# A Mamba scan between two expert layers: sum of state 14 one step earlier on TensorE, low parts of the projected rows one state later on VectorE

## The chip, the cores and the metric

The kernel runs on one core of a Trainium2 chip. The metric is the device time of one execution in microseconds; lower is better. Five engines work side by side, each through its own list of instructions in order: TensorE (PE; its weight loads are shown as PEld), VectorE (DVE), ScalarE (ACT), GpSimd (POOL) and SyncE (SP, which only starts transfers). They meet through semaphores.

## The reference

A block of three layers on x of 32 sequences x 256 tokens x 128 values, in float32: a mixture of 8 experts (two chosen for each token), a two-way Mamba layer, and the mixture again. The Mamba layer is the part that matters here. It is computed once forward and once on the flipped sequence, with weights of its own:

```python
xz = x @ in_w.T
xi, z = split(xz, 2)                       # 256 channels each
xc = silu(conv1d_depthwise(xi, 4 taps) + conv_b)
x_dbl = xc @ xp_w.T                        # dt (8), B (16), C (16)
delta = softplus(dt @ dtp_w.T + dtp_b)
# for each of 16 states n, over time t:
h[n] = h[n] * exp(delta * A[n]) + (delta * xc) * B[n]
y = sum over n of h[n] * C[n] + xc * Dp
out = (y * silu(z)) @ out_w.T
```

## The kernel before

The first expert layer (`moe(0)`), the Mamba stage and the second expert layer (`moe(1)`) follow one another. The Mamba stage is cut into 16 pairs `p` of two sequences each. A pair has two units: r=0 forward and r=1 backward; unit number u = 2p + r. A unit works on 256 channels (two halves c of 128 partitions) x 512 columns (2 sequences x 256 tokens), and on 16 states n, one after another. Each engine has a loop over the 16 states with the work of a state, and beside it, at fixed places of its list, the preparation of the next unit and the end of the one before. These places are tables at the top of the file: `DVE_AT`, `POOL_AT`, `ACT_AT`, `PE_AT`, `CONV_AT`, `SUM_AT`, keyed by the state at which the engine is. A whole number is behind that state's own work, a half one after the item of the whole number.

For each state n of a unit:

- ACT makes the decay exp(delta * A[n]) (`decay`, L1164; `decay_to_bank`, L1174, for the states 3, 9 and 15), three states ahead.
- The product delta * xc * B[n] comes from one of three ways. For the states 3, 9 and 15 POOL makes it (`product`, L535); for 2, 4, 6, 8, 10, 12 and 14 ACT scales a transposed copy (`scale_by_B`, L1197) and PE turns it back (`turn_back`, L1522); for 0, 1, 5, 7, 11 and 13 PE spreads the row B[n] over all partitions (`spread`, L1489) and DVE multiplies (`product`, L889).
- DVE runs the recurrence (`scan`: L917, or L904 for 3, 9 and 15).
- POOL multiplies with C[n] (`times_C`, L548) into one of four buffers `hC`. State N waits there until PE has summed state N - 4.
- PE adds the result to the unit's sum in banks 4 and 5 (`sum_states`, L1547, eight transposing matmuls), which ends by raising `y_done`.

When all 16 sums are done, DVE multiplies with silu(z) (`gate`, L877); `gate` waits for `y_done` of state 15. It stands behind the scan of state 2 of the next unit (`DVE_AT["gate"] = 2`).

`SUM_AT` says at which step of PE a state is summed; keys from 16 on are steps 0, 1, 2 of the next unit. Before, key 18 holds the states 14 and 15. `CONV_AT` puts the taps of the next unit's convolution (L1422) between: one tap of c=1 at 1.6 and two at 2.0, which stand ahead of the sums of step 2.

PE's list at step n is: turn back state n + 1, spreads, the items of n, the sums of n, a spread, the items of n + 0.5 and n + 0.6.

The preparation of the next unit goes: convolution (PE), silu (ACT, L1125), projection of z (PE, L1432), projection to dt, B and C into bank 6 (PE, `project_x`, L1454, at 4.5), their high parts (ACT, `split_hi`, L1135, at 3.5) and their low parts (DVE, `split_lo`, L864), rows that make float32 out of two shortened numbers; then the step size (PE, `project_dt`, L1465, at 8.5). `split_lo` waits for the high parts. `project_dt` and the spread of state 0 of the next unit wait for the low parts. Before, `DVE_AT["lo"]` is 5.5: behind the scan of state 5.

```python
def split_lo(p, r):
    dve.wait_ge(s["act_pre"], done(ACT_PRE, f"hi{r}", p))
    V.tensor_tensor(BCs[r][LOW:ROWS, :], bank[6][LOW:ROWS, :], ...)
def gate(u, r):
    dve.wait_ge(s["y_done"], (u + 1) * NS)
```

Of the kernel before, what the change touches and what calls it, by code (L numbers as in the profile page):

```python
# [39 lines left out]
ACT_NORM = ["xn", "xnT", "xnTrev"]  # L40


DVE_AT = {"stats": 2.5, "gate": 2, "sum": 5.5, "lo": 5.5, "size": 10.5}
POOL_AT = {"rstd": 1, "du": 9}
ACT_AT = {"xn": 3.0, "silus": 2.0, "xnT": 6.5, "hi": 3.5, "BT": 8.0, "parts": 8.5, "ln": 9.0, "gT": 12.0,
    "duT0": 12.5, "duT1": 14.5, "res": 13.5}
PE_AT = {"z": 3.0, "skip": 4, "xdbl": 4.5, "xt": 6.0, "BT": 8.0, "dt": 8.5, "gT": 11.5, "out0": 12.5,
    "out1": 12.5, "duT0": 12.5, "duT1": 14.0}
CONV_AT = {0.0: (0, 3, 1), 0.6: (1, 0, 1), 1.6: (1, 1, 1), 2.0: (1, 2, 2), 14.0: (0, 0, 2), 15.0: (0, 2, 1)}
SUM_AT = {6: (0, 1, 2), 7: (3, 4), 9: (5, 6), 11: (7, 8), 12: (9,), 13: (10,), 15: (11,), 16: (12, 13), 18: (14,  # L50
    15)}
SP_AT = {"rows": 8}
EARLY, Y_BUFS = 10, 3

# [70 lines left out]
def macaron_kernel(nc, x, gateT, wgT, wuT, wdT, inT, xpT, dtpT, chan, outT, ident, tri, e_rank,  # L125
# [38 lines left out]
    with ExitStack() as ctx:  # L164
# [414 lines left out]
        def _(dve):  # L579
# [268 lines left out]
            def layernorm(p):  # L848
                wait(dve, s["act_norm"], done(ACT_NORM, "xn", p - 1))
                dve.wait_ge(s["comb_done"], p + 1)  # L850
                dve.sem_inc(s["aggr_turn"], 1)
                for t in range(G):
                    ins = V.bn_stats(st[:, t, :], X[:, bass.ds(p * G + t, 1), :])
                ins.then_inc(s["dve_norm"], 1)
                dve.wait_ge(s["dve_norm"], done(DVE_NORM, "stats", p))
                dve.sem_inc(s["aggr_turn"], 1)
                for t in range(G):
                    ins = V.bn_aggr(MV[:, t, :], st[:, t, :])
                ins.then_inc(s["dve_norm"], 1)

            def split_lo(p, r):

                dve.wait_ge(s["act_pre"], done(ACT_PRE, f"hi{r}", p))
                V.tensor_tensor(BCs[r][LOW:ROWS, :], bank[6][LOW:ROWS, :], BCs[r][LOW:ROWS, :].bitcast(F32),  # L864
                                ALU.subtract).then_inc(s["dve_pre"], 1)

            def step_size(p, r):

                dve.wait_ge(s["act_pre"], done(ACT_PRE, f"ln{r}", p))
                V.scalar_tensor_tensor(out=delta[r], in0=pairs[3][:, :], scalar=0.0, in1=tmp, op0=ALU.max,  # L870
                                       op1=ALU.add).then_inc(s["dve_pre"], 1)

            def gate(u, r):
                dve.wait_ge(s["y_done"], (u + 1) * NS)
                wait(dve, s["pe_post"], 2 * u)
                for h in range(S):
                    ins = V.tensor_tensor(gat[:, h * W:(h + 1) * W], bank[4 + h], zs[r][:, h * W:(h + 1) * W], ALU.mult)  # L877
                ins.then_inc(s["gated"], 1)
# [12 lines left out]
            def scan(p, r, n):  # L891

                u = p * 2 + r
                N = u * NS + n
                b = n % R
                wait(dve, s["hC_ready"], N + 1 - R)
                if on_pool(n):
                    turn = pool_before(u, n)
                    dve.wait_ge(s["pool_mul_done"], turn + 1)
                    for c in range(C):  # L900
                        dve.wait_ge(s[f"dP_ready{c}"], turn + 1)
                        for q in range(S):
                            w = slice(c * W + q * L, c * W + (q + 1) * L)
                            ins = V.tensor_tensor_scan(hs[:, b, w], bank[c][:, q * L:(q + 1) * L],  # L904
                                                       prod[:, turn % 2, w], 0.0, ALU.mult, ALU.add)
                        ins.then_inc(s[f"scan_done{c}"], 1)
                    return
                dve.wait_ge(s["dA_ready"], decays_before(u, n) + 1)
                for c in range(C):
                    w = slice(c * W, (c + 1) * W)  # L910
                    if on_turn(n):
                        dve.wait_ge(s[f"turned{c}"], turned_before(u, n) + 1)
                        source = turned_bank(n, c)
                    else:
                        dve.wait_ge(s["mul_done"], 2 * vector_before(u, n) + c + 1)
                        source = bank[c]
                    V.tensor_tensor_scan(hs[:, b, w], dA[:, b, c, :, :].rearrange("p s t -> p (s t)"),  # L917
                                         source, 0.0, ALU.mult, ALU.add).then_inc(s[f"scan_done{c}"], 1)

            def pair(p, first, last):  # L920
                for r in range(2):
# [3 lines left out]
                    for n in range(NS):  # L925
                        scan(p, r, n)
                        if n == DVE_AT["gate"] and not (first and r == 0):
                            gate(u - 1, 1 - r)
                        if prep and n == DVE_AT["lo"]:
                            split_lo(pv, rv)  # L930
# [5 lines left out]
                        if not prep:  # L936
                            continue
                        if n + 0.5 == DVE_AT["lo"]:
                            split_lo(pv, rv)
                        if n + 0.5 == DVE_AT["size"]:  # L940
                            step_size(pv, rv)
                        if r == 0 and not last and n + 0.5 == DVE_AT["stats"]:
                            layernorm(p + 1)
# [325 lines left out]
        def _(pe):  # L1269
# [270 lines left out]
            def sum_states(p, r, n):  # L1540

                N = p * 2 * NS + r * NS + n
                pe.wait_ge(s["hC_ready"], N + 1)
                for q in range(G):
                    for c in range(C):
                        at = (q % 2) * DI + c * P
                        ins = M.matmul(bank[4 + q // 2][:, at:at + P],  # L1547
                                       hC[:, n % R, c * W + q * P:c * W + (q + 1) * P], id_sb[:, :], is_transpose=True,
                                       start=False, stop=(n == NS - 1), skip_group_check=True)
                ins.then_inc(s["y_done"], 1)  # L1550

            def sums(p, r, n, first):
                for m in SUM_AT.get(n + NS, ()):
                    if not (first and r == 0):
                        sum_states(p if r else p - 1, 1 - r, m)
                for m in SUM_AT.get(n, ()):
                    sum_states(p, r, m)
# [77 lines left out]
            for n in range(NS, NS + NS // 2):  # L1635
                for m in SUM_AT.get(n, ()):
                    sum_states(NP - 1, 1, m)
# [70 lines left out]
```

## Time and profile before

| | us |
|---|---|
| median of 3 runs | 2614.42 (2611.18 to 2614.97) |
| profiled execution | 2614.2 |
| its span, first to last instruction | 2612.1 |
| busy in the span: PE / DVE / ACT / POOL | 2227.8 / 2240.6 / 1895.3 / 2198.4 |
| stretch 1000 to 1400, in the Mamba stage: POOL / DVE / ACT / PE busy | 392.2 / 388.6 / 368.6 / 350.5 |

An engine is idle when its next instruction waits. The profile names what ended the wait, and its line. "issue" is idle time in which the profile shows no other instruction that was waited for; a semaphore of a transfer or of an engine whose instruction had ended a moment before can stand behind it. In a timeline, instructions of one form that follow one another are merged (x4), and the column after "us" is the length of the whole piece. Ends of matmuls are modelled, so the starts are what one goes by.

### The profile page before, as it was taken

What the parts mean: (1) busy time and instruction counts of PE and PEld (TensorE: products, weight loads), DVE (VectorE), ACT (ScalarE), POOL (GpSimd) and SP (SyncE); (2) the same over time, 40 slices, a digit from 0 to 9 for tenths busy, and PEclk for the clock granted to TensorE, in tenths of its full rate; (3) what the DMA queues carried; (4) which work ended last, traced back from release to release, by engine and by line L of the source; (5) the groups of instructions that cost most, each with busy time, mean ns of one, the idle gap of its engine ahead of it and who ended that gap; (6) DMA issues with size and microseconds to landing.
All of it is one profiled execution on the core that took longest, in us unless ns stands there. A gap on an engine that the chain in (4) does not pass through costs nothing.

```text
span 2612.1 us, 48904 instructions
## 1 busy us (share of the span) xinstructions
PE 2227.8 (85%) x15840; PEld 1908.7 (73%) x15840; DVE 2240.6 (86%) x3430; ACT 1895.3 (73%) x3628; POOL 2198.4 (84%) x1402
## 2 busy tenths in 40 slices
PE   4899999668888898888888888888988768999992
PEld 3799999446776777776776766766766647999992
DVE  8766666789999999999999999999999887666666
ACT  4355555389999989999999999999999543555551
POOL 3677777379999999999999999999999936777772
PEclk8999999889999999999999999999999978999996
DMA  7011112533333333333333333333333240111126
GB/s 249 21 48 49 49 50 50 144 94 105 110 103 104 107 106 102 107 107 101 111 101 103 112 100 105 111 107 104 106 107 107 85 161 24 50 49 49 49 49 211
DMA packets 156821, 248.73 MB, mean 95 GB/s; under 512 B 22082, under 2 KB 66018, under 8 KB 155874
## 3 DMA queue, kind: packets, MB, share of 16 engines
q1 hardware_dynamic: 137568, 202.79, 26.1%
q0 software_dynamic: 18208, 37.26, 5.3%
q10 hardware_dynamic: 866, 6.43, 0.6%
q8 instruction: 96, 1.57, 0.2%
q14 instruction: 83, 0.68, 0.1%
HBM read 213.10 MB, written 33.29 MB: 94 GB/s over the span
## 4 chain that ended last, share of the span: by engine, by line
PE 37%; POOL 19%; DVE 15%; issue 14%; ACT 10%; DMA 4%; ACTq 0%; DVEq 0%; POOLq 0%; SPq 0%
PE bank L1351 10%; POOL buf L548 8%; DVE buf L917 7%; PE bank L1547 6%; PE bank L1372 6%; PE bank L1422 4%; POOL token_outputs L497 4%; POOL buf L487 4%; PE bank L1522 3%; PE bank L1332 3%; ACT over L1164 3%; DMA buf<-state_rows 2%; ACT scaled L1197 2%; DVE buf L904 2%; POOL buf L535 2%
## 5 line engine op out<-in xcount | busy, mean ns | idle before, releaser
L548 POOL TENSOR_TENSOR buf<-buf 128x1024 f32<-128x1024 f32 x512 | 1199.9, 2374 | 32.4 <-PE bank L1547 27.0
L917 DVE TENSOR_TENSOR_SCAN buf<-over,bank 128x512 f32<-128x512 f32 x832 | 953.8, 1200 | 4.9 <-PE bank L1522 2.7
L1164 ACT ACTIVATE over<-wgu,negA 128x510 f32<-128x510 f32 x832 | 541.5, 709 | 40.3 <-DVE buf L917 28.8
L1547 PE MATMUL bank<-id_sb,buf 128*128 128x128 f32 x4096 | 515.8, 279 | 6.8 <-POOL buf L548 6.8
L1547 PEld LDWEIGHTS bank<-id_sb,buf 128*128 128x128 f32 x4096 | 478.2, 144 | 57.2 <-issue 46.6
L1351 PE MATMUL bank<-parts 128*128 128x256 f32 x3408 | 447.6, 288 | 17.3 <-DVE buf L767 9.2
L1351 PEld LDWEIGHTS bank<-parts 128*128 128x128 f32 x3408 | 420.7, 193 | 36.7 <-issue 36.7
L1197 ACT ACTIVATE scaled<-wd_sb,I 128x256 f32<-128x256 f32 x896 | 377.3, 497 | 22.6 <-PE bank L1522 22.5
L497 POOL DMA_INDIRECT token_outputs<-buf,slot_out x284 | 299.5, 1055 | 87.9 <-issue 84.0
L487 POOL DMA_INDIRECT buf<-token_rows,slot_token x284 | 284.5, 1002 | 95.4 <-issue 82.5
L1522 PE MATMUL bank<-id_sb,scaled 128*128 128x128 f32 x1792 | 256.0, 280 | 88.3 <-ACT scaled L1197 38.2
L1522 PEld LDWEIGHTS bank<-id_sb,scaled 128*128 128x128 f32 x1792 | 202.8, 142 | 166.8 <-issue 69.3
L1372 PE MATMUL bank<-buf 128*128 128x128 f32 x2272 | 276.3, 275 | 1.1 <-ACT buf L1065 1.1
L1372 PEld LDWEIGHTS bank<-buf 128*128 128x128 f32 x2272 | 265.6, 192 | 1.5 <-issue 1.5
L764 DVE TENSOR_TENSOR parts<-wgu,parts 128x512 fp32r<-128x512 f32 x284 | 183.9, 689 | 88.3 <-ACT parts L1052 53.8
L889 DVE TENSOR_TENSOR bank<-wgu,bank 128x512 f32<-128x512 f32 x384 | 243.5, 680 | 8.8 <-PE bank L1489 6.4
L1422 PE MATMUL bank<-buf 128*128 128x512 f32 (+3 forms) x512 | 248.1, 599 | 1.2 <-ACT buf L1119 1.2
L1065 ACT ACTIVATE buf<-bank 128x256 f32<-128x256 f32 x142 | 54.7, 385 | 266.0 <-DMA token_outputs<-buf,slot_out 169.9
L904 DVE TENSOR_TENSOR_SCAN buf<-bank,buf 128x256 f32<-128x256 f32 x384 | 231.7, 666 | 10.0 <-issue 9.5
L535 POOL TENSOR_TENSOR buf<-wgu,buf 128x1024 f32<-128x1024 f32 x96 | 228.3, 2379 | 0.0
L753 DVE TENSOR_TENSOR parts<-bank,parts 128x256 fp32r<-128x256 f32 x142 | 60.3, 425 | 168.6 <-ACT parts L1042 162.0
L776 DVE TENSOR_TENSOR buf<-buf,bank 128x512 f32<-128x512 f32 x284 | 180.5, 674 | 10.3 <-PE bank L1351 9.2
(170 smaller groups left out, 3061.6 us busy)
## 6 DMA issues: line engine op xcount, KB each, us to landing
buf<-state_rows SPq DMA_DIRECT2D x608, 256.0 KB, 3.2
token_rows<-buf SPq DMA_DIRECT2D x32, 256.0 KB, 2.3
wd_sb<-token_outputs SPq DMA_DIRECT2D x16, 512.0 KB, 4.0
buf<-token_outputs SPq DMA_DIRECT2D x16, 512.0 KB, 4.8
buf<-token_rows,slot_token POOLq DMA_INDIRECT x284, 2.5
token_outputs<-buf,slot_out POOLq DMA_INDIRECT x284
out<-X SPq DMA_DIRECT2D x16, 256.0 KB, 3.6
wgu<-wgT ACTq DMA_DIRECT2D x1, 2048.0 KB, 9.1
```

The lines of the kernel that those rows point to most:

```text
L487: pool.indirect_dma_start(out=xin[:, i % X_BUFS, h, :], out_offset=None, in_=xn_rows[:, :], in_offset=bass.IndirectOffsetOnAxis(ap=slot_to ...
L497: pool.indirect_dma_start(out=yt[:, :], out_offset=bass.IndirectOffsetOnAxis(ap=slot_out[:, i * HT + h:i * HT + h + 1], axis=0), in_=yo[:, ...
L548: pool.tensor_tensor(hC[:, b, :].rearrange("p (c w) -> p c w", c=C), hs[:, b, :].rearrange("p (c w) -> p c w", c=C), Cs[:, b, :].unsqueeze ...
L904: ins = V.tensor_tensor_scan(hs[:, b, w], bank[c][:, q * L:(q + 1) * L], prod[:, turn % 2, w], 0.0, ALU.mult, ALU.add)
L917: V.tensor_tensor_scan(hs[:, b, w], dA[:, b, c, :, :].rearrange("p s t -> p (s t)"), source, 0.0, ALU.mult, ALU.add).then_inc(s[f"scan_don ...
L1164: ins = A.activation(dA[:, n % R, c, :, 1:], delta[r][:, c * W:(c + 1) * W].rearrange("p (s t) -> p s t", s=S)[:, :, 1:], ACT.Exp, scale=n ...
L1197: ins = A.activation(scaled[:, turned_before(u, n) % 2, q, :], duT[:, q, :], ACT.Copy, scale=BT[:, u % 2, q, n:n + 1])
L1351: ins = M.matmul(bk[:, c * TP:(c + 1) * TP], w[:, b, cols], xx[:, b, :], start=(j == 0), stop=(j == 2))
L1372: ins = M.matmul(bank[7][:, h * D:(h + 1) * D], hid[:, b, c * TP + h * P:c * TP + (h + 1) * P], wd_e[:, q, c * D:(c + 1) * D], start=(c == ...
L1422: ins = M.matmul(acc[:, :, j:], tapW[:, r, KW - 1 - j, c * P:(c + 1) * P], xnT[:, r, :, 0:L - j], start=(j == 0), stop=(j == KW - 1), skip ...
L1522: ins = M.transpose(turned_bank(n, c)[:, q * P:(q + 1) * P], scaled[:, turned_before(u, n) % 2, q, c * P:(c + 1) * P], id_sb[:, :])
L1547: ins = M.matmul(bank[4 + q // 2][:, at:at + P], hC[:, n % R, c * W + q * P:c * W + (q + 1) * P], id_sb[:, :], is_transpose=True, start=Fa ...
```

## The change

Two tables are edited. The sum of state 14 goes from step 18 to step 17 of TensorE's list, behind the turning back of state 2 and ahead of three taps of the convolution; the sum of state 15 stays at step 18. The low parts go from 5.5 to 6.5 in VectorE's list, that is, behind the scan of state 6 and the product of state 7. The entry "sum" of `DVE_AT`, which no line reads, is taken out.

```diff
-DVE_AT = {"stats": 2.5, "gate": 2, "sum": 5.5, "lo": 5.5, "size": 10.5}
+DVE_AT = {"stats": 2.5, "gate": 2, "lo": 6.5, "size": 10.5}
...
-SUM_AT = {6: (0, 1, 2), 7: (3, 4), 9: (5, 6), 11: (7, 8), 12: (9,), 13: (10,), 15: (11,), 16: (12, 13), 18: (14,
-    15)}
+SUM_AT = {6: (0, 1, 2), 7: (3, 4), 9: (5, 6), 11: (7, 8), 12: (9,), 13: (10,), 15: (11,), 16: (12, 13), 17: (14,),
+    18: (15,)}
```

## Rows read from the trace of the kernel before

**Rows 1.** Busy us (instructions) of PE, PEld, DVE, ACT, POOL, clock, DMA: stretches, sum.
```profile
1135.73:1183.25 47.52, 41.55 (x285) 33.46 (x284) 46.20 (x54) 44.23 (x82) 46.60 (x20) 1.00 0.40 107
...
sum 96.36, PE 84.04 PEld 67.29 DVE 93.89 ACT 88.76 POOL 94.89; mean PE 42.02 PEld 33.65 DVE 46.94 ACT 44.38 POOL 47.44
```

**Rows 2.** Groups by line, 560 to 2040 us: busy, mean ns, idle before, releasers.
```profile
L548 POOL TENSOR_TENSOR buf<-buf 128x1024 f32<-128x1024 f32 x492 | 1153.1, 2375 | 21.5 <-PE bank L1547 19.9 <-DVE buf L917 1.5
...
L877 DVE TENSOR_TENSOR buf<-bank,wgu 128x512 f32<-128x512 f32 x60 | 38.7, 687 | 17.9 <-PE bank L1547 17.9
```

**Rows 3.** Timeline of POOL: start, length, instruction, count, idle before in brackets.
```profile
1135.73 2.38 POOL L548 TENSOR_TENSOR buf<-buf 128x1024 f32<-128x1024 f32 x1 [0.20 <-PE bank L1547]
...
1159.03 2.38 POOL L535 TENSOR_TENSOR buf<-wgu,buf 128x1024 f32<-128x1024 f32 x1
...
1173.00 2.36 POOL L535 TENSOR_TENSOR buf<-wgu,buf 128x1024 f32<-128x1024 f32 x1
...
1183.25 2.38 POOL L548 TENSOR_TENSOR buf<-buf 128x1024 f32<-128x1024 f32 x1 [0.92 <-PE bank L1547]
```

**Rows 4.** Timeline of DVE, the same pair of units.
```profile
1135.80 0.69 DVE L864 TENSOR_TENSOR BCs<-bank,BCs 40x512 fp32r<-40x512 f32 x1 [0.41 <-ACT BCs L1135]
...
1161.49 2.43 DVE L904 TENSOR_TENSOR_SCAN buf<-bank,buf 128x256 f32<-128x256 f32 x4
...
1167.26 1.26 DVE L889 TENSOR_TENSOR bank<-wgu,bank 128x512 f32<-128x512 f32 x2
1168.44 4.55 DVE L917 TENSOR_TENSOR_SCAN buf<-over,bank 128x512 f32<-128x512 f32 x4
1173.58 1.29 DVE L877 TENSOR_TENSOR buf<-bank,wgu 128x512 f32<-128x512 f32 x2 [0.59 <-PE bank L1547]
1175.45 2.43 DVE L904 TENSOR_TENSOR_SCAN buf<-bank,buf 128x256 f32<-128x256 f32 x4 [0.58 <-issue]
...
1183.56 0.69 DVE L864 TENSOR_TENSOR BCs<-bank,BCs 40x512 fp32r<-40x512 f32 x1
1184.29 2.33 DVE L917 TENSOR_TENSOR_SCAN buf<-over,bank 128x512 f32<-128x512 f32 x2
1186.53 1.27 DVE L889 TENSOR_TENSOR bank<-wgu,bank 128x512 f32<-128x512 f32 x2
```

**Rows 5.** Timeline of PE, the same unit.
```profile
1167.91 1.33 PE L1522 MATMUL bank<-id_sb,scaled 128*128 128x128 f32 x8
1169.08 2.72 PE L1422 MATMUL bank<-buf 128*128 128x510 f32 x6
1171.64 1.91 PE L1547 MATMUL bank<-id_sb,buf 128*128 128x128 f32 x16
...
1179.14 0.47 PE L1489 MATMUL bank<-BCs,sel 104*128 104x512 f32 x1 [1.05 <-DVE buf L917]
...
1182.04 2.78 PE L1547 MATMUL bank<-id_sb,buf 128*128 128x128 f32 x24
1185.65 0.47 PE L1489 MATMUL bank<-BCs,sel 104*128 104x512 f32 x1 [0.83 <-DVE buf L917]
...
1191.05 0.47 PE L1465 MATMUL bank<-BCs,dtp_high 104*128 104x512 f32 x1 [0.44 <-ACT I L1180]
```

**Rows 6.** Short timelines: POOL's products with C of 13, 14; PE in the unit r=0.
```profile
1163.70 4.69 POOL L548 TENSOR_TENSOR buf<-buf 128x1024 f32<-128x1024 f32 x2
...
1211.20 4.69 POOL L548 TENSOR_TENSOR buf<-buf 128x1024 f32<-128x1024 f32 x2
...
1216.69 2.72 PE L1422 MATMUL bank<-buf 128*128 128x510 f32 x6
```

**Rows 7.** Timeline of ACT: the table load ahead of the silus.
```profile
1172.28 1.28 ACT L1125 ACT_TABLE_LOAD   x1
```

**Rows 8.** Last unit: a spread on PE and the product on DVE that waited for it.
```profile
2054.37 0.49 PE L1489 MATMUL bank<-BCs,sel 104*128 104x512 f32 x1
...
2054.89 1.29 DVE L889 TENSOR_TENSOR bank<-wgu,bank 128x512 f32<-128x512 f32 x2 [0.49 <-PE bank L1489]
```

## The prediction

> **What bounds the kernel now.** I read the stages first, then one pair of units, then the idle times by line, and last the timelines of the engines over one pair. The change touches only the Mamba stage, from 545 to 2087, some 1540 of the 2612.1 us of the span. In it a pair of units takes 96.36 us, POOL (GpSimd) is busy for 94.89 of them, DVE (VectorE) for 93.89, PE (TensorE) for 84.04, at a granted clock of 1.00 in its unit r=1 [rows 1]. So POOL bounds the stage, and DVE is one microsecond behind: a gain has to shorten POOL's idle time, and a loss on DVE soon counts.
>
> POOL's idle time has one place: 21.5 us in 560:2040, nearly all ahead of L548 [rows 2]. The timeline shows which instruction that is: the product with C of state 4, once in a unit, 0.20 us in the unit r=0 and 0.92 us in the unit r=1 [rows 3]. It waits for PE's sum of state 0 (it takes over that buffer). Going back from the 0.92: the sums 0 to 2 start at 1182.04 and take 2.61, so the first is done near 1182.9; PE had waited for DVE at 1179.14, by a spread that waits for the scan of state 4 [rows 5]; DVE had started the scan of state 3 at 1175.45 [rows 4], 0.09 us after POOL's own product of state 3 ended (1173.00 + 2.36 = 1175.36) [rows 3]. In the unit r=1 the circle is thus POOL, DVE, PE, POOL, and neither the gate nor the low parts are in it: the gate ends at 1173.58 + 1.29 = 1174.87, and DVE then stands for 0.58 us. In the unit r=0, with layernorm behind the gate, DVE is the later one, and the gate is in the chain. That unit leaves POOL 0.20 us to win, no more.
>
> **Part 1, sum 14 one step earlier.** Before, PE's order is: turn back state 2, three taps of the convolution, sums 14 and 15, turn back state 4. After it: turn back state 2, sum 14, three taps, sum 15. Nothing is added. The gate waits for sum 15 for 0.59 us, in 30 gates of two instructions, 17.9 us in 560:2040 [rows 2, 4]. What sets that time: PE's turning back of state 2 takes 1.33 us instead of the usual 1.04, as its second half waits for DVE's product of state 1, which ends at 1167.26 + 1.26 = 1168.52; from there PE needs some 0.1 + 0.44 for the half, 1171.64 - 1169.08 = 2.56 for the taps, 1.74 for two sums and 0.2 for the handover, and gives 1173.58; DVE's own scans 1 and 2 are through at 1172.99 [rows 4, 5]. All three pieces still stand between the product of state 1 and the gate. Their order changes, their sum doesn't: gain 0.
>
> The new wait: sum 14 at its new place wants POOL's product with C of state 14. That ends at 1163.70 + 4.69 = 1168.39, and PE gets there at 1169.08, so 0.69 us are left; in the unit r=0 it is 1211.20 + 4.69 = 1215.89 against 1216.69, 0.80 us [rows 6]. A handover from POOL costs 0.09 (above). The distance is stable, since both sides start from one event: POOL's product of state 15 ends at 1159.03 + 2.38 = 1161.41, DVE starts the scan of state 15 at 1161.49, and the product of state 1 follows from there without a gap. Cost 0. If that cover were gone, the taps, sum 15, the gate and the turning back of state 4 would be queued behind the waiting sum. The taps end one sum later, 0.87 us, at 1172.5; their reader, the silu on ScalarE, comes after a table load that ends at 1172.28 + 1.28 = 1173.56 [rows 7], so cost 0. The buffer of sum 14 comes free 2.6 us earlier, but POOL has no idle ahead of state 2 that could use it [rows 3].
>
> At this place a rule of the Trainium skill could speak against the change. The row first: eight transposing matmuls of a sum followed by taps run without a toll (the next group starts 8 x 0.109 = 0.87 us after the first, as within a block of 16) [rows 5]. "TensorE: Matmul & The Clock Gate", section "Single matmul latency", gives a lone matmul a fixed part of some 166 ns at the warm clock, which a stream hides. If each of the two new changes of group paid that, an estimate from the page alone, the gate would come 0.33 us later; by the rows it is 0, and the sum takes 0.
>
> **Part 2, low parts of the rows one state later.** Before: scan 5, low parts, scan 6, product 7, scan 7. After: scan 5, scan 6, product 7, low parts, scan 7. In the unit r=0 the low parts waited 0.41 us for ScalarE's high parts, at 1135.80 [rows 4]; the wait is there in 14 units r=0. Moved behind 2.3 + 1.2 us of other work, that wait goes. What is late next: DVE gets as far as the scan of state 15, which starts 0.08 us after POOL's product of that state ends, so nearly the whole 0.41 turns into a wait there; what passed would end at the scan of state 3 in the next unit, which stands 0.58 us for POOL anyway [rows 3, 4]. Value between 0 and 14 x 0.41 = 5.7 us; I take 0, as two rows stand in its way.
>
> In the unit r=1 the low parts had no wait, and DVE is busy without a gap from scan 3 to the next gate, so a stall that the new order made there would pass through that gate to POOL. Scan 6 and product 7 now want their inputs 0.73 us earlier (the step of 1183.56 to 1184.29), product 7 at 1185.80 instead of 1186.53. It needs PE's spread of state 7, which was at 1185.65 after an idle time of 0.83 [rows 4, 5], so it can follow to 1184.92, 0.10 us after PE is free. From a spread to a product that waited for it are 0.52 us (2054.37 to 2054.89) [rows 8]; product 7 could start at 1185.44, 0.36 us ahead of need. Cost 0, from 0 to 0.73 a unit if I read that wrongly. The low parts themselves end where product 7 ended before, near 1187.7; their readers are the step-size projection, at 1191.05 and held by ScalarE, not DVE [rows 5], and the spread of state 0 of the next unit, later still. 3.3 us of cover: cost 0.
>
> **Sum.** 0 + 0 on POOL's path. The profiled execution took 2614.2 us (span 2612.1 and 2.1 around it), 0.2 below the median of the three runs. Forecast: 2614.2 us.
>
> **Rivals.** (1) Faster by the low parts: DVE keeps the 0.41 us of each unit r=0 and the stage ends sooner by 14 x 0.41 = 5.7: 2608.5. For it: DVE is busy for 93.89 of 96.36. Against it: the two places where DVE meets POOL. A near relative is that the gate comes earlier by up to its 0.59: POOL's wait in units r=0, mostly 0.2, then goes, some 15 x 0.2 = 3 us, 2611, inside "no change". (2) Slower by the new place of sum 14: PE finds POOL's product 14 unfinished. It decides once PE arrives 0.7 us earlier against POOL than the rows show. A stall of 0.5 us costs nothing in units r=1 (0.58 to spare at scan 3) but the whole in units r=0: 15 x 0.5 = 7.5, so 2622. (3) Slower by the low parts: the spread of state 7 doesn't come earlier, product 7 starts where it did and the low parts come on top, 0.73 in each of 15 units r=1: 2625; half of it 2620. It decides when PE is over 0.46 us (0.10 + 0.36) late there. (4) That the change doesn't do what it says: that sum 15, the last, is what the gate waits for, and it isn't moved. That is my forecast's reason as well.
>
> **How the numbers follow.** A measurement of this kernel can tell about 0.2%, 5.2 us, from no change. No change: 0.69. Rival 1 at its full size: 0.14. Rivals 2 and 3: 0.10 and 0.07. The range goes from rival 1 to a little over rival 2, 2608 to 2623, which leaves out the full rival 3 and gains of other kinds.
>
> **What would show it.** After: POOL's waits at state 4 as before, about 0.2 and 0.92; the gate's wait of 0.59 still there with PE's order turned; no wait at L864; in its stead some 0.4 us of idle at DVE's L904 in units r=0 (state 15). PE without idle ahead of sum 14. I'd be wrong if L1547 or L1489 gained waits on POOL or DVE, if L889 waited for L1489, or if POOL's idle total left 21.5 by more than 5.

## The result

The changed kernel is slower. Its median is 2622.76 us (2619.46 to 2624.17, 7 runs) against 2613.69 us of the kernel before (2610.17 to 2614.97, 7 runs): a ratio of 1.0035, 95% interval 1.0023 to 1.0046, some 9 us. The forecast was no change at 2614.2 us. The time lies just inside the range of 2608 to 2623, but the direction is wrong. The profiled execution took 2620.12 us, its span 2618.0; that is 5.9 us over the profiled execution before, so the traces show two thirds of the 9 us.

The page of the changed kernel, first the busy times, then TensorE's granted clock in 40 slices:

```profile
PE 2248.6 (86%) x15840; PEld 1929.6 (74%) x15840; DVE 2242.5 (86%) x3430; ACT 1895.4 (72%) x3628; POOL 2198.7 (84%) x1402
...
PEclk8999999889999999999999999999999878999996
```

The number of instructions is the same and so is the work of DVE, ACT and POOL, but PE is busy for 20.8 us more (2248.6 against 2227.8). The same matmuls took longer. The mean granted clock of the whole span fell from 0.962 to 0.952 (0.947 to 0.949 in the other six runs).

One pair of units shows where. Stretches from gate to gate, columns as in [rows 1]; first the kernel before, then the changed one with the same pair and with the pair ahead of it:

```profile
738.15:786.91 48.76, 42.22 (x288) 33.90 (x287) 47.52 (x63) 45.48 (x85) 47.96 (x25) 1.00 0.34 105
786.91:834.54 47.63, 41.86 (x284) 33.42 (x283) 46.37 (x55) 43.30 (x79) 46.70 (x21) 1.00 0.36 107
```

```profile
738.23:787.56 49.33, 43.53 (x288) 35.43 (x287) 47.59 (x62) 45.56 (x85) 48.68 (x25) 0.97 0.33 104
787.56:835.12 47.56, 43.12 (x284) 35.05 (x283) 46.46 (x55) 43.16 (x79) 46.62 (x21) 0.96 0.39 107
641.89:690.63 48.74, 42.11 (x288) 33.88 (x287) 47.58 (x62) 45.45 (x85) 47.56 (x25) 1.00 0.40 104
690.63:738.23 47.60, 41.81 (x284) 33.41 (x283) 46.36 (x55) 43.29 (x79) 46.68 (x21) 1.00 0.35 107
```

The changed kernel needs 96.34 us for its pair at clock 1.00, as the one before does (96.39 here). Where the clock is 0.97 and 0.96, the same pair takes 96.89. So the new order is as fast as the old one, and something makes the clock fall.

The timeline of PE in the unit r=0 of that pair, around the step-size projection (L1465):

```profile
751.12 0.63 PE L1522 MATMUL bank<-id_sb,scaled 128*128 128x128 f32 x4 [0.18 <-issue]
752.33 0.66 PE L1522 MATMUL bank<-id_sb,scaled 128*128 128x128 f32 x4 [0.58 <-DVE bank L889]
752.82 1.91 PE L1547 MATMUL bank<-id_sb,buf 128*128 128x128 f32 x16
754.79 0.39 PE L1498 MATMUL bank<-id_sb,bc_out 16*128 16x16 f32 x4
757.35 0.47 PE L1465 MATMUL bank<-BCs,dtp_high 104*128 104x512 f32 x1 [2.16 <-ACT I L1180]
...
758.43 1.91 PE L1522 MATMUL bank<-id_sb,scaled 128*128 128x128 f32 x8
760.14 2.66 PE L1547 MATMUL bank<-id_sb,buf 128*128 128x128 f32 x16
762.56 0.47 PE L1489 MATMUL bank<-BCs,sel 104*128 104x512 f32 x1
```

The same place in the kernel before, where the idle time is in four pieces:

```profile
751.22 0.47 PE L1489 MATMUL bank<-BCs,sel 104*128 104x512 f32 x1 [0.59 <-DVE buf L917]
752.29 0.63 PE L1522 MATMUL bank<-id_sb,scaled 128*128 128x128 f32 x4 [0.60 <-DVE buf L917]
753.42 0.66 PE L1522 MATMUL bank<-id_sb,scaled 128*128 128x128 f32 x4 [0.51 <-DVE bank L889]
...
757.27 0.47 PE L1465 MATMUL bank<-BCs,dtp_high 104*128 104x512 f32 x1 [1.09 <-ACT I L1180]
...
758.28 1.04 PE L1522 MATMUL bank<-id_sb,scaled 128*128 128x128 f32 x8
```

And the changed kernel's stretch in pieces of one to three microseconds (columns as in [rows 1], the granted clock is the third from the end):

```profile
754.00:757.00 3.00, 1.12 (x11) 0.81 (x9) 3.00 (x4) 3.00 (x6) 3.00 (x2) 1.00 0.01 2
757.00:758.00 1.00, 0.65 (x3) 0.59 (x4) 1.00 (x2) 1.00 (x4) 1.00 (x1) 1.00 0.58 156
758.00:759.00 1.00, 1.00 (x6) 0.79 (x5) 1.00 (x3) 1.00 (x3) 1.00 (x2) 0.63 0.45 123
759.00:760.00 1.00, 1.00 (x7) 1.00 (x6) 1.00 (x3) 0.97 (x2) 1.00 (x1) 0.50 0.25 86
...
762.00:763.00 1.00, 1.00 (x9) 0.72 (x7) 0.13 (x1) 1.00 (x3) 1.00 (x1) 1.00 0.58 180
```

PE stands idle for 2.16 us in one piece, waiting for ACT's copy of the columns of B. Right behind it the clock is 0.50, that is 1.2 instead of 2.4 GHz, and the turning back of state 10 takes 1.91 us instead of 1.04, the sums of 5 and 6 take 2.66 instead of 1.91. The spread of state 11 comes behind these, and DVE waits for it:

```profile
763.07 1.29 DVE L889 TENSOR_TENSOR bank<-wgu,bank 128x512 f32<-128x512 f32 x2 [0.94 <-PE bank L1489]
```

Counted in stretches of one microsecond, the clock fell 12 times between the first and the 31st gate of the kernel before (some 1.7 us of clock time lost in each fall) and 25 times in the changed one. A stretch at 0.50 that is twice as long counts as two falls. Before, ten of the twelve came 12 to 16 us behind a gate; now nearly all come 17 to 20 or 23 to 24 us behind it. The stage between these two gates grew from 1447.9 to 1454.3 us. These 6.4 us cover the whole difference of the two profiled executions (5.9 us).

Groups by line, 560 to 2040 us, of the changed kernel (see [rows 2]), then three of the kernel before:

```profile
L548 POOL TENSOR_TENSOR buf<-buf 128x1024 f32<-128x1024 f32 x489 | 1145.7, 2376 | 23.9 <-PE bank L1547 21.9 <-DVE buf L917 2.0
...
L889 DVE TENSOR_TENSOR bank<-wgu,bank 128x512 f32<-128x512 f32 x366 | 232.8, 681 | 15.5 <-PE bank L1489 15.5
...
L567 POOL TENSOR_TENSOR wgu<-wgu 128x1024 f32<-128x1024 f32 x31 | 73.8, 2380 | 5.1 <-DVE wgu L870 4.5
...
L877 DVE TENSOR_TENSOR buf<-bank,wgu 128x512 f32<-128x512 f32 x60 | 38.6, 686 | 18.0 <-PE bank L1547 18.0
...
L1465 PE MATMUL bank<-BCs,dtp_high 104*128 104x512 f32 x62 | 30.2, 488 | 53.0 <-ACT I L1180 53.0
...
L864 DVE TENSOR_TENSOR BCs<-bank,BCs 40x512 fp32r<-40x512 f32 x30 | 20.9, 695 | 0.9
```

```profile
L889 DVE TENSOR_TENSOR bank<-wgu,bank 128x512 f32<-128x512 f32 x369 | 233.9, 680 | 2.9 <-PE bank L1489 2.9
...
L567 POOL TENSOR_TENSOR wgu<-wgu 128x1024 f32<-128x1024 f32 x31 | 73.8, 2381 | 0.0
...
L1465 PE MATMUL bank<-BCs,dtp_high 104*128 104x512 f32 x62 | 26.8, 433 | 19.8 <-ACT I L1180 19.8
```

PE's idle time ahead of the projection went from 19.8 to 53.0 us, DVE's waits for a spread from 2.9 to 15.5. The last step, to POOL, shows in two groups. DVE makes the step size (L870) right behind the product of state 11, and POOL waits for it ahead of its product of step size and input (L567): 4.5 us, where it had waited for nothing. And POOL's waits ahead of L548 grew from 21.5 to 23.9. So only a part of DVE's 12.6 us more reaches the engine that bounds the stage.

### The profile page after: what moved, and what is told of

Read it like the earlier page. It is cut to its first block, busy times and chain, and to the rows that moved or that the text cites. A ratio compares the mean times of both kernels' runs of the same rounds, so it can differ in the third digit from the quotient of the medians.

```text
span 2618.0 us, 48904 instructions
## 1 busy us (share of the span) xinstructions
PE 2248.6 (86%) x15840; PEld 1929.6 (74%) x15840; DVE 2242.5 (86%) x3430; ACT 1895.4 (72%) x3628; POOL 2198.7 (84%) x1402
## 3 DMA queue, kind: packets, MB, share of 16 engines
q8 instruction: 96, 1.57, 0.2%
## 4 chain that ended last, share of the span: by engine, by line
PE 50%; DVE 15%; ACT 13%; issue 11%; POOL 8%; DMA 2%; ACTq 0%; DVEq 0%; POOLq 0%; SPq 0%
PE bank L1351 12%; PE bank L1547 8%; PE bank L1422 7%; DVE buf L917 7%; PE bank L1372 7%; ACT over L1164 5%; PE bank L1522 4%; ACT scaled L1197 3%; PE bank L1332 3%; POOL token_outputs L497 3%; PE bank L1432 2%; POOL buf L487 2%; DVE bank L889 2%; PE bank L1474 2%; POOL buf L548 2%
## 5 line engine op out<-in xcount | busy, mean ns | idle before, releaser
L548 POOL TENSOR_TENSOR buf<-buf 128x1024 f32<-128x1024 f32 x512 | 1199.4, 2375 | 34.5 <-PE bank L1547 28.9
L1547 PE MATMUL bank<-id_sb,buf 128*128 128x128 f32 x4096 | 526.0, 281 | 6.2 <-POOL buf L548 6.2
L1547 PEld LDWEIGHTS bank<-id_sb,buf 128*128 128x128 f32 x4096 | 486.6, 146 | 55.8 <-issue 46.3
L1522 PE MATMUL bank<-id_sb,scaled 128*128 128x128 f32 x1792 | 272.1, 290 | 69.7 <-DVE bank L889 34.2
L1522 PEld LDWEIGHTS bank<-id_sb,scaled 128*128 128x128 f32 x1792 | 213.5, 147 | 153.6 <-issue 68.2
L889 DVE TENSOR_TENSOR bank<-wgu,bank 128x512 f32<-128x512 f32 x384 | 244.3, 681 | 21.0 <-PE bank L1489 18.6
```

What stands on the lines that cost most here:

```text
L548: pool.tensor_tensor(hC[:, b, :].rearrange("p (c w) -> p c w", c=C), hs[:, b, :].rearrange("p (c w) -> p c w", c=C), Cs[:, b, :].unsqueeze ...
L889: V.tensor_tensor(bank[c], du[r][:, c * W:(c + 1) * W], B_bank[vector_before(0, n) % 2], ALU.mult).then_inc(s["mul_done"], 1)
L1522: ins = M.transpose(turned_bank(n, c)[:, q * P:(q + 1) * P], scaled[:, turned_before(u, n) % 2, q, c * P:(c + 1) * P], id_sb[:, :])
L1547: ins = M.matmul(bank[4 + q // 2][:, at:at + P], hC[:, n % R, c * W + q * P:c * W + (q + 1) * P], id_sb[:, :], is_transpose=True, start=Fa ...
```

## The experiments

**The table.** The kernels ran on different chips. On one sort the kernel before takes some 2614 us, on the other 2792 to 2810, nearly all of the difference in the expert layers; so each is compared with the kernel before on its own chip. "Falls" and "stage" are of one profiled execution, between the first and the 31st gate. The kernel before was profiled on one chip only, so its 12 and 1447.9 serve for all; the two executions of the changed kernel, 25 and 29 falls, show how far the number moves by itself.

| kernel | us | before, same chip | ratio (95%) | mean clock, before | falls | stage us |
|---|---|---|---|---|---|---|
| before | 2613.69 | | | 0.962 (profiled) | 12 | 1447.9 |
| changed | 2622.76 | 2613.69 | 1.0035 (1.0023-1.0046) | 0.948 | 25 | 1454.3 |
| e8 changed again | 2621.84 | 2614.83 | 1.0029 (1.0018-1.004) | 0.947, 0.960 | 29 | 1454.8 |
| e1 low parts only | 2799.54 | 2791.74 | 1.0018 (1.0006-1.003) | 0.946, 0.956 | 28 | 1454.9 |
| e2 sum 14 only | 2791.14 | 2791.74 | 0.9996 (0.9985-1.0006) | 0.955, 0.956 | 12 | 1449.4 |
| e5 low parts at 6 | 2618.43 | 2614.83 | 1.0014 (1.0005-1.0023) | 0.953, 0.960 | 17 | 1448.4 |
| e7 before, fewer sums | 2618.49 | 2614.83 | 1.0013 (1.0004-1.0022) | 0.944, 0.960 | 31 | 1448.8 |
| e3 changed + zeros | 2794.64 | 2791.74 | 1.0008 (0.9996-1.002) | 0.956, 0.956 | 11 | 1448.3 |
| e6 changed + more zeros | 2610.64 | 2614.83 | 0.9983 (0.9974-0.9992) | 0.967, 0.960 | 0 | 1443.8 |
| e10 low parts only + more zeros | 2788.28 | 2794.24 | 0.9981 (0.9971-0.999) | 0.964, 0.957 | 0 | 1443.7 |
| e4 before + zeros | 2795.48 | 2791.74 | 1.0012 (1.0001-1.0023) | 0.954, 0.956 | 14 | 1451.7 |
| e9 before + more zeros | 2791.47 | 2794.24 | 0.9991 (0.9982-1.0001) | 0.961, 0.957 | 5 | 1445.0 |
| e11 before, sum 0 early | 2801.26 | 2810.32 | 0.9969 (0.9957-0.9982) | 0.944, 0.949 | 18 | 1438.9 |
| e12 changed + zeros, sum 0 early | 2796.96 | 2810.32 | 0.9951 (0.9937-0.9965) | 0.955, 0.949 | 8 | 1434.8 |

**Which part is it?** e1 moves the low parts only, e2 sum 14 only.

```diff
-DVE_AT = {"stats": 2.5, "gate": 2, "sum": 5.5, "lo": 5.5, "size": 10.5}
+DVE_AT = {"stats": 2.5, "gate": 2, "lo": 6.5, "size": 10.5}
```

> Only the low parts are moved (5.5 to 6.5), both sums stay at step 18. Theory (clock): with the low parts later, scan 6, product 7, the spread of 7 and the turning back of 8 come earlier, PE collects its idle time in one piece ahead of the step-size projection (2.16 us in units r=0, 1.29 in units r=1 in the changed kernel, against 1.09 and 0.44 before), its granted clock falls behind that piece, and the spread of state 11 and the product of state 11 come late. It expects the whole loss here: about 9 us over the kernel before, a mean granted clock near 0.948, DVE's L889 waiting for L1489 some 15 us. Rival (sum): the loss comes from sum 14 at its new place, and here the time is that of before, within 3 us.

```diff
-SUM_AT = {... 16: (12, 13), 18: (14, 15)}
+SUM_AT = {... 16: (12, 13), 17: (14,), 18: (15,)}
```

> Only sum 14 is moved to step 17, the low parts stay at 5.5. Theory (clock through the low parts): within 3 us of before, mean granted clock near 0.962, idle ahead of the step-size projection 1.09 and 0.44 as before. Rival (sum): 9 us slower, with the taps and sum 14 in the new order the place where PE's time goes.

e1 has the whole longer stage of the changed kernel (1454.9 us), 28 falls, and lost 7.8 us; e2 has the falls of before, a median 0.6 us below it, and a stage of 1449.4 us in its slowest execution. The loss belongs to the low parts, and sum 14 at its new place costs nothing.

The changed kernel itself, run again on the chip of e5 to e7, loses the same as at first:

> The changed kernel as it is, to have it on the same chip as the others: slower than before by 5 to 10 us, mean granted clock 0.006 to 0.014 below before's.

**Is it the order or the clock?** If the order by itself held PE up, more work on PE could only make it worse. e3 puts matmuls of zeros into the idle piece; they add zero to the running sum.

```diff
+    M.matmul(bank[4][:, 0:256], id_sb[:, :], zero_sb[:, 0:1].broadcast_to([P, 256]), start=False, stop=False, ...)
...
 if prep and at == PE_AT["dt"]:
+    add_zeros(4 if r == 0 else 2)
     project_dt(pv, rv)
```

> The changed kernel, and in the idle piece of PE ahead of the step-size projection matmuls that add zeros to bank 4 (four of 256 columns in units r=0, two in units r=1, some 0.43 us each, so 1.7 and 0.9 us of the 2.16 and 1.29): more work on PE, nothing computed differently, no wait changed. Theory (clock): the clock no longer falls behind that piece, the product of state 11 finds its row, time back to that of before or a few us below it (2606 to 2615), mean granted clock above 0.96. Rival (order alone: the new order of DVE's list makes PE late by itself, whatever the clock): time stays near 2622 or grows by what the zeros cost. Second rival (it is the sum): stays near 2622 too.

The stage is back at 1448.3 us, with 11 falls instead of 25 to 29. The ratio to before is 1.0008, against 1.0018 (e1, same chip) to 1.0035 without the zeros. The intervals of e3 and e1 overlap, so this step rests on the falls and on the stage, 6.6 us shorter than e1's. Most of the loss is gone, not all of it: the expectation was missed by a little, in the time (2.9 us above before, not at or below it) and in the clock (0.956, as before on this chip, not above 0.96). Its timeline says why, with the falls that are left:

```profile
746.04 0.39 PE L1500 MATMUL bank<-id_sb,bc_out 16*128 16x16 f32 x4
746.36 2.00 PE L1506 MATMUL bank<-zero_sb,id_sb 128*128 128x256 f32 x8
748.60 0.47 PE L1467 MATMUL bank<-BCs,dtp_high 104*128 104x512 f32 x1 [0.23 <-ACT I L1182]
...
754.46 1.44 PE L1530 MATMUL bank<-id_sb,scaled 128*128 128x128 f32 x8 [1.57 <-ACT scaled L1199]
755.70 3.27 PE L1555 MATMUL bank<-id_sb,buf 128*128 128x128 f32 x16
```

The zeros fill the old piece; the next idle piece, 1.57 us ahead of the turning back of state 12, is now followed by a fall (two sums in 3.27 us). e6 fills that one too, and the one ahead of the spread of state 5.

```diff
+if n + 1 == 12:
+    add_zeros(3 if r == 0 else 1)
 if on_turn(n + 1):
     turn_back(p, r, n + 1)
...
+if n == 4 and r == 0:
+    add_zeros(3)
```

> The changed kernel with zeros added in three idle pieces of PE: ahead of the spread of state 5 (three of 256 columns in units r=0), ahead of the step-size projection (four and two) and ahead of the turning back of state 12 (three and one). Theory (clock): the falls left in the kernel with zeros at one place came behind the idle piece ahead of the turning back of 12 (1.57 us), so they go too: a pair of units takes 96.3 us throughout, falls in the Mamba stage at most 5, time 2 to 5 us below before on the same chip. Rival (order alone): zeros only add work, time at or above the changed kernel's.

No fall is left in the stage, each pair but the last takes 96.3 to 96.6 us, DVE waits for no spread any more, and the kernel beats the one before (0.9983) with more work on PE. It is 11.2 us below the changed kernel on the same chip.

**The other way round: less work.** e7 is the kernel before, the low parts at their old place, with the sums of states 3 and 4 halved.

```diff
-for q in range(G):
+for q in range(2 if n in (3, 4) else G):
```

> The kernel before (low parts at 5.5, sums as before) with work taken away: the sums of states 3 and 4 are done for half of the time blocks only, so the sums of those two states are incomplete. PE does 0.87 us less per unit just ahead of the step-size projection and stands idle there for 0.87 us more (some 1.9 and 1.3 us). Theory (clock): the clock falls in most units as in the changed kernel, and the kernel with less work is slower than before, by 3 to 9 us. Rival (order alone): less work on PE, nobody waits longer: same time or faster.

```profile
756.73 0.41 PE L1498 MATMUL bank<-id_sb,bc_out 16*128 16x16 f32 x4
759.11 0.47 PE L1465 MATMUL bank<-BCs,dtp_high 104*128 104x512 f32 x1 [1.96 <-ACT I L1180]
...
760.11 1.74 PE L1522 MATMUL bank<-id_sb,scaled 128*128 128x128 f32 x8
```

The idle piece is 1.96 us, the clock falls behind it, 31 falls in all. So idle time and falls come with the low parts at their old place too, by taking work away. The kernel is 3.7 us slower, but only a part of it is what the theory said. The profiled executions are 4.3 us apart: 0.9 of that lies in the stage between the gates, 1.3 ahead of the first gate and 2.1 behind the 31st, all of it behind the last gate, where the second expert layer follows, whose code is the same. Near its start 50 us run at a mean clock of 0.77 (2093.81 to 2143.81) instead of 0.84 (2091.64 to 2141.64 before), and why isn't shown. DVE's waits for a spread grew by 6.1 us, but little of that reached POOL, whose idle time ahead of L567 is 0.9 us. The stretch 700 to 2030 us of four kernels (before, changed, e6, e7):

```profile
700.00:2030.00 1330.00, 1166.17 (x7829) 943.68 (x7826) 1293.52 (x1591) 1221.19 (x2228) 1306.21 (x603) 0.99 0.36 106
```

```profile
700.00:2030.00 1330.00, 1177.85 (x7782) 955.79 (x7779) 1288.97 (x1584) 1216.31 (x2219) 1299.74 (x601) 0.97 0.36 105
```

```profile
700.00:2030.00 1330.00, 1239.23 (x8208) 990.90 (x8206) 1297.02 (x1598) 1223.90 (x2237) 1309.68 (x605) 1.00 0.35 106
```

```profile
700.00:2030.00 1330.00, 1165.80 (x7601) 940.36 (x7600) 1292.96 (x1590) 1221.25 (x2227) 1303.93 (x604) 0.96 0.36 105
```

e7 does 228 matmuls fewer than before and its PE is busy as long; e6 does 379 more and POOL, the bound, is busy for 3.5 us more of the same 1330. POOL's busy time in a fixed stretch says roughly how much of the work got done in it: 1299.7 in the changed kernel, 1303.9 in e7, 1306.2 before, 1309.7 in e6.

**How much of the move is needed?** e5 puts the low parts between scan 6 and product 7.

```diff
-"lo": 5.5
+"lo": 6
```

> The kernel before with the low parts half a state later only: behind scan 6, ahead of product 7. Product 7, and with it the second half of PE's turning back of state 8, then stay where they were in units r=1 and come 0.4 us earlier in units r=0. Theory (clock, through PE running ahead of ScalarE): idle ahead of the step-size projection stays 0.44 in units r=1 and grows to some 1.5 us in units r=0, so fewer falls of the clock than with 6.5 and a time within 4 us of before. Rival (any later place of the low parts costs, through their readers): 4 us slower or more.

17 falls, idle ahead of the projection 29.3 us (19.8 before, 53.0 changed), 3.6 us slower. Falls and idle time lie between the two. The stage hardly moved (1448.4 against 1447.9), so most of these 3.6 us lie outside it, as with e7. The ratio fits "within 4 us" and nearly the rival's "4 or more", so it doesn't tell the two apart by itself.

**Is the old order better or worse once the clock holds?**

```diff
 if prep and at == PE_AT["dt"]:
+    add_zeros(2 if r == 0 else 1)
```

> The kernel before, with the same zeros at the same place, two in units r=0 and one in units r=1 (0.86 and 0.43 us of idle 1.09 and 0.44). Theory (clock): the clock falls that before has left, 12 of its 30 units, come in part behind other idle pieces (ahead of the spread of 7 and the turning back of 8), so a small gain or none: 2606 to 2614, fewer falls than before. Rival (order alone): no gain, 2614 to 2617 as the zeros cost time.

A miss: 14 falls, the stage 3.8 us longer, 3.7 us slower. In the kernel before, the falls come ahead of the place that these zeros fill, behind the idle pieces at the spread of 7 and the turning back of 8; that it got worse, not just no better, I can't explain from its trace. With zeros in four places (ahead of the spreads of 5 and 7, of the projection and of the turning back of 12):

> The kernel before with zeros in four idle pieces of PE (matmuls of 256 columns, units r=0 / r=1): ahead of the spread of state 5 (3 / 1), of state 7 (1 / 1), of the step-size projection (2 / 1), of the turning back of state 12 (2 / 1). If both orders are equal once the clock holds (my theory), it comes out as the changed kernel with zeros did: 0.1 to 0.25% below before, a pair of units at 96.3 us, mean clock near 0.967. If the new order has a gain of its own that the clock hid, this kernel stays 2 us or more above the changed one with zeros. If zeros cost time where the clock didn't fall, it is slower than before.

Five falls, four of them still 14 us behind a gate, a stage of 1445.0, and 2.8 us below before (0.09%, where 0.1 to 0.25% was expected); the interval just takes in no change. And the changed kernel with zeros but sum 14 back at 18:

> The changed kernel with zeros in three places, but sum 14 back at step 18. Theory (sum 14's place is worth nothing): within 2 us of the changed kernel with zeros in three places, so 0.1 to 0.25% below before, with the gate's wait of 0.6 us unchanged. Rival (the sum's place helps the gate or hurts the taps): 3 us or more away from it.

No fall, 1443.7 us, the same as e6's 1443.8: sum 14's place is worth 0.1 us in 1444. Between e9 and e10 are 3.2 us on one chip, with 5 and 0 falls; pairs without a fall take 96.3 to 96.6 us in both. So a pair takes the same in both orders when the clock holds. The expectation of e9 had set 2 us as the sign of a gain of the new order's own, and 3.2 is over it. 1.3 us of it lie in the stage and go with the falls (1445.0 against 1443.7); the rest lies outside the stage, and as the intervals of e9 and e10 overlap, it decides nothing.

**The bound, tested.** If POOL's waits for the sum of state 0 bound a pair, that sum should be earlier.

```diff
-SUM_AT = {6: (0, 1, 2),
+SUM_AT = {4: (0,), 6: (1, 2),
```

> The kernel before with the sum of state 0 at step 4 instead of 6, in the idle piece of PE ahead of the spread of state 5. It tests the reading of what bounds a pair of units: POOL's waits at state 4 (0.92 us in units r=1, 0.20 and more in units r=0) end with the sum of state 0. If that reading holds, both waits go and a pair shrinks from 96.4 towards POOL's own 95.2, some 15 us over the stage, less what falls of the clock do now that PE's idle time moves: 5 to 15 us below before. Rival (DVE with its gate and PE behind it are as tight): the wait turns up at the gate or the scan of state 3, gain under 3 us.

> The changed kernel with zeros in PE's idle pieces (one, four/two, three/one of 256 columns) and the sum of state 0 at step 4. Both theories together: no falls of the clock in the Mamba stage and no wait of POOL at state 4, 10 to 20 us below before on the same chip. If the clock falls again since the idle pieces have moved, it comes out within 3 us of the kernel before with the sum of state 0 early.

Both times are as expected: 9.1 and 13.4 us below before. But e12 was to have no falls in the stage, and it has 8. POOL's idle time ahead of L548 in 640 to 2130 us, e11 and e12:

```profile
L548 POOL TENSOR_TENSOR buf<-buf 128x1024 f32<-128x1024 f32 x495 | 1159.0, 2379 | 3.5 <-DVE buf L917 1.9 <-PE bank L1547 1.5
```

```profile
L550 POOL TENSOR_TENSOR buf<-buf 128x1024 f32<-128x1024 f32 x496 | 1162.4, 2387 | 2.5 <-DVE buf L919 1.5 <-PE bank L1555 0.9
```

e11 gained although its clock fell more often than before's (18 falls). e12 has the lowest ratio to before of all, 0.9951.

## Why the prediction was wrong, step by step

**Part 1, sum 14: right.** The order in the changed kernel:

```profile
781.96 1.27 PE L1522 MATMUL bank<-id_sb,scaled 128*128 128x128 f32 x8
783.06 1.04 PE L1547 MATMUL bank<-id_sb,buf 128*128 128x128 f32 x8
783.93 2.72 PE L1422 MATMUL bank<-buf 128*128 128x510 f32 x6
786.49 1.04 PE L1547 MATMUL bank<-id_sb,buf 128*128 128x128 f32 x8
787.36 1.04 PE L1522 MATMUL bank<-id_sb,scaled 128*128 128x128 f32 x8
```

There is no wait ahead of sum 14, and each sum of eight takes 0.87 us from its start to that of the next group (783.06 to 783.93, 786.49 to 787.36), as within a block. The fixed part of a lone matmul that the Trainium skill gives in "TensorE: Matmul & The Clock Gate", section "Single matmul latency", isn't paid at these changes of group. The gate waits 0.60 us as before (18.0 us in sum). e2 and the pair e6, e10 give 0 for this part.

**Part 2, DVE's side: right.** The wait at L864 is gone, and in units r=0 at full clock DVE waits for POOL at the scan of state 15 in its stead:

```profile
678.54 2.43 DVE L904 TENSOR_TENSOR_SCAN buf<-bank,buf 128x256 f32<-128x256 f32 x4 [0.36 <-issue]
```

Product 7 lost nothing in units r=1, and POOL's wait at state 4 of a unit r=1 is 0.93 us.

**Part 2, PE's side: the step that failed.** "Scan 6 and product 7 now want their inputs 0.73 us earlier" was followed to the spread of 7 and stopped there. The same move lets PE do the turning back of 8, the sums of 3 and 4 and the turning of B 0.7 us earlier, and ACT, which it then waits for, had not moved. I gave the reader of the low parts 3.3 us of cover and booked "cost 0"; the projection did start on time. But PE's idle time, spread over four short pieces (0.59, 0.60, 0.51 and 1.09 us in units r=0), became 0.18, 0.58 and 2.16 us: later and in one piece. Nobody waits for an idle PE, so I gave idle time no price. Its price is the clock behind it: 10.5 us of stage for 25 falls in the changed kernel, measured against e6, which has none, and 4.1 us for the 12 falls of the kernel before. That is some 0.4 us a fall, and the term that the sum lacked is the 13 falls more, 6.4 us of stage. The sign named for being wrong, L889 waiting for L1489, came true: 15.5 us. The price is no constant: against e6, the 31 falls of e7 cost 5.0 us, 0.16 each, and the 14 of e4 cost 7.9, 0.56 each. What a fall costs seems to depend on how much of DVE's wait gets through to POOL (here some 4.5 + 2.4 of 12.6 us); no run isolates that. Of the 9 us between the medians some 3 lie outside what the two traces show; in the trace of e8, 7.9 us over that of before, the stage has 6.9.

**The forecast rested on one pair.** "At a granted clock of 1.00 in its unit r=1" [rows 1] was true of the pair that I read. The stage before had 12 falls, and its stretches of 200 and 240 us between 560 and 2040 us have means of 0.97 to 1.00; that was the sign that the clock already fell here and there. Neither of the two slower rivals was it, though 2622 and 2620 lie close to the measured time, and it is luck that the range, which ends just over rival 2, takes it in: the spread that came late was that of state 11, not 7, and it came late by PE's speed, not by its order.

**The reading of the bound: right.** e11 took most of POOL's waits at state 4 away (3.5 us are left ahead of L548) and gained 9.1 us, in its range of 5 to 15.

A rule of the Trainium skill bears on the cause. "TensorE: Matmul & The Clock Gate", section "HAM oscillation — how this bites in real kernels", says that waits of TensorE inside a loop let its clock fall, and that each pass then begins slowly. The traces agree in kind: clock 0.50 right behind the idle piece of 2.16 us, and none of it once this piece and two more are filled (e6). They differ in size: the waits of the section's kernel are longer than 2.16 us, and here that much was enough. What exactly makes the clock fall behind one piece and not behind another of the same length, and with it why two executions of the same kernel have 25 and 29 falls, stays open here.

## What to carry to other kernels

When an edit makes an engine's input come earlier, follow that engine to its next wait and ask what its idle time becomes: for TensorE, idle time gathered into one piece can cost a fall of the clock and the work behind it, even where nobody waits for the engine and where the order without the fall is as good as before. Read the granted clock over the whole stage, not of one clean pair, before booking such an edit at nothing. And if the clock already falls here and there, work of no use in the idle pieces is a cheap test, at times a cheap gain (here 0.17%; with the sum of state 0 early 0.5%, of which that sum alone gave 0.3%). At the wrong place it is a loss (e4, 0.12%).

## What was not expected of the hardware

- A kernel with 228 matmuls fewer in 1330 us keeps PE busy as long, falls 31 times instead of 12 and is 3.7 us slower (e7; 0.9 of it in the stage), and one with 379 more is 4.2 us faster (e6; 4.1 in the stage).
- Falls of 1.7 us of clock time each are priced by where they land: 0.2 us of stage a fall in e7, 0.4 in the changed kernel (each against e6's stage). e7 has less work on PE and is not a clean measure of it.
- Zeros at one place of the kernel before made it 3.7 us slower, at four places 2.8 us faster: filling one idle piece can move the falls without removing any (14 against 12).
